# Four of eight heads of the projection as three fp32r products in two of the four slots, with their inputs split on GpSimd, ScalarE and VectorE

## The reference

```python
# branch 1, on the layernorm of x; 16 heads of width 64, INNER = 1024
h1 = adaln(x, t, norm1_w, norm1_b)
x = mha(h1, h1, attn1_wq, attn1_wk, attn1_wv, attn1_wo, attn1_bo) + x
h2 = adaln(x, t, norm2_w, norm2_b)
x = mha(h2, context, attn2_wq, attn2_wk, attn2_wv, attn2_wo, attn2_bo) + x
h3 = adaln(x, t, norm3_w, norm3_b)
x = glu_ff(h3, ff_w1, ff_b1, ff_w2, ff_b2) + x
# mha: q, k, v = projections; out = softmax(q k^T / 8) v per head; out @ wo + bo
# branch 2, on the layernorm of the sum: 8 experts, two per token
out_token = sum(score[e] * (silu(a_e) * g_e @ w2[e].T) for e in top2)
```

## Time and profile before

| | us |
|---|---|
| three runs | 2203.51, 2203.67 (median), 2211.51 |
| the profiled execution | 2204.38 |
| its span | 2202.6 |
| TensorE busy | 2084.2 (95%) |
| ScalarE busy | 1387.8 (63%) |
| VectorE busy | 1283.3 (58%) |
| GpSimd busy | 826.0 (38%) |
| projection, f32 passes (two a head) | 1024 of mean 594 ns |
| granted clock of TensorE over the span | 0.985 |

### The profile page before, as it was taken

One profiled execution on the slowest core, in us unless ns is written; L12 is line 12 of the kernel. 1 busy time (PEld: TensorE's weight loads), 2 busy tenths in 40 slices (PEclk: granted clock), 3 DMA queues, 4 the chain that ended last, 5 costly groups with the idle time before them and its releaser, 6 DMA issues. The chain is left out here.

```text
span 2202.6 us, 37962 instructions
## 1 busy us (share of the span) xinstructions
PE 2084.2 (95%) x11004; PEld 1328.8 (60%) x11004; DVE 1283.3 (58%) x3373; ACT 1387.8 (63%) x2629; POOL 826.0 (38%) x1022
## 2 busy tenths in 40 slices
PE   6899999999999999999999999999999797898896
PEld 5455555555555555555555555555555466788896
DVE  4454656565656565666666665666554744455465
ACT  4566666676757676767675767676666555565564
POOL 1222323334343433342424333333323443556653
PEclk9999999999999999999999999999999898999998
DMA  4110111111111212112121111211114111112256
GB/s 141 48 27 25 49 34 49 49 49 44 48 50 45 59 34 57 45 46 53 38 53 42 49 48 47 59 41 50 39 35 118 43 53 43 51 50 63 61 178 207
DMA packets 134576, 127.73 MB, mean 58 GB/s; under 512 B 14665, under 2 KB 108521, under 8 KB 134442
## 3 DMA queue, kind: packets, MB, share of 16 engines
q1 hardware_dynamic: 125162, 108.03, 17.6%
q0 software_dynamic: 9280, 18.28, 2.5%
HBM read 86.63 MB, written 40.67 MB: 58 GB/s over the span
## 5 line engine op out<-in xcount | busy, mean ns | idle before, releaser
L1795 POOL TENSOR_TENSOR pr<-pr,sm 128x512 f32<-128x512 f32 x256 | 264.3, 1047 | 812.9 <-DVE sm L1355 812.9
L775 PE MATMUL ps<-tt,V 128*128 128x512 f32 x1024 | 502.2, 594 | 3.5 <-ACT tt L1050 3.5
L1050 ACT ACTIVATE kp<-ps 128x512 f32<-128x512 f32 x512 | 294.5, 600 | 198.8 <-PE ps L272 196.1
L1345 DVE TENSOR_REDUCE mx<-ps 128x8 f32<-128x512 f32 x256 | 176.9, 691 | 347.0 <-PE ps L732 346.9
L1050 ACT ACTIVATE tt<-ps 128x512 f32<-128x512 f32 x512 | 275.3, 591 | 42.5 <-PE ps L762 42.2
L732 PE MATMUL ps<-kp,hf 128*64 128x256 f32 x2048 | 279.2, 394 | 14.2 <-DVE pr L1348 11.1
L272 PE MATMUL ps<-cT,M 128*128 128x512 f32 x768 | 267.9, 472 | 0.0
L272 PE MATMUL ps<-hk,M 128*128 128x512 f32 x768 | 249.1, 447 | 1.9 <-DVE hk L1404 1.9
L732 PEld LDWEIGHTS ps<-kp,hf 128*64 128x64 f32 x2048 | 125.5, 137 | 205.4 <-DVE pr L1348 141.0
L1050 ACT ACTIVATE pt<-ps 128x512 f32<-128x512 f32 x256 | 153.7, 600 | 149.9 <-PE ps L744 147.3
L877 PE MATMUL ps<-xT,wt 128*128 128x128 f32 (+1 forms) x1728 | 226.0, 282 | 16.6 <-DVE ux L1610 7.6
(11 more groups left out here) (219 smaller groups left out, 3032.5 us busy)
## 6 DMA issues: line engine op xcount, KB each, us to landing
mod<-emb_s SPq DMA_DIRECT2D x96, 256.0 KB, 4.2
xr<-rows_s SPq DMA_DIRECT2D x144, 66.0 KB
cb<-y_s SPq DMA_DIRECT2D x32, 256.0 KB, 5.1
x_in<-in_x_dram SPq DMA_DIRECT2D x16, 256.0 KB, 4.3
xn_s<-x_in SPq DMA_DIRECT2D x16, 256.0 KB, 2.0
res<-xn_s SPq DMA_DIRECT2D x16, 256.0 KB, 2.7
c_in<-in_ctx_dram SPq DMA_DIRECT2D x16, 256.0 KB, 4.7
y_s<-res SPq DMA_DIRECT2D x16, 256.0 KB, 2.1
```

What stands on the lines that cost most here:

```text
L775: mm = nc.tensor.matmul(psO[:], Vw[a][:, g * HG + head_at(h), :], tt[:, h, :], start=(g == 0 and h == 0), stop=(g == 1 and h == HG - 1))
L1050: return nc.scalar.activation(o, i, ACT.Copy)
L1345: nc.vector.tensor_reduce(mx[:, p % 2, :], heads(psS[p % 2][:]), AX_X, ALU.max).then_inc(max_done, 1)
L1795: tensor(v, v, sm[:, p, :].unsqueeze(2).broadcast_to([P, HG, 64]), ALU.mult).then_inc(prob_done, 1)
```

## The change

Of the eight heads of a unit the last four (HF = 4, HR = 4) become three fp32r products, for units 3 and 0 (RU) only. In the setup their V is stored as hi and lo (Vr) instead of f32. The weighted sums of these heads are split into tt_h and tt_l, 128x4x128 a pair: pairs 0 to 2 by GpSimd (split: a multiplication by ones that writes fp32r, then a subtraction), pair 3 by ScalarE (last_split, behind the second key) and VectorE (last_rest). The split heads are projected in the slot after the unit's, that is in slots 0 and 1. The rest of the change makes room: a semaphore less for the router (rt_rec counts both), for the zero rows (st_rows begins at DM) and for combine (cb_done counts both sums), and the table tb1 lies in the memory of tb2.

```diff
+    HF = HG // 2
+    HR = HG - HF
+            RU = (3, 0)
+            R0 = sa("R0", [P, 2, HR, D], F32R)
+            R3 = sa("R3", [P, 2, HR, D], F32R)
+            Mw, Vw, Vr = [M0, M1], [V0, V1], {0: R0, 3: R3}
+                tt_h, tt_l = (sw(f"tt_{k}", [P, HR, CT], F32R) for k in "hl")
...
# TensorE, project
+                ends = g == 1 and h == HG - 1
+                if u in RU and h >= HF:
+                    if h == HF:
+                        pe.wait_ge(tr_lo, 3 * split_seq(i, u) + 3)
+                        pe.wait_ge(last_lo, split_seq(i, u) + 1)
+                    halves = tt_h[:, h - HF, :], tt_l[:, h - HF, :]
+                    mm = mm3(psO[:], lambda k: Vr[u][:, k, h - HF, :], lambda k: halves[k], first=False, last=ends)
+                else:
+                    mm = nc.tensor.matmul(psO[:], Vw[a][:, g * HG + head_at(h), :], tt[:, h, :], start=(g == 0 and h == 0), stop=ends)
...
# ScalarE: setup copy of a V tile of these units, and the last pair
+                    if unit in RU:
+                        at, src = 2 * (g % 2), ps[:].rearrange("p (a two b) -> p a two b", a=2, two=2)
+                        copy(Vw[a][:, 8 * (g // 2) + g % 2:8 * (g // 2) + 8:4, :], src[:, :, 0, :])
+                        op = copy(Vr[unit][:, 0, at:at + 2, :], src[:, :, 1, :])
+            def last_split(i, u):
+                act.wait_ge(tt_done, t_count(i, u, 3))
+                copy(tt_h[:, :, 3 * P:], tt[:, HF:HG, 3 * P:]).then_inc(last_hi, 1)
+                    if h == 1 and last and lu in RU:
+                        last_split(li, lu)
...
# VectorE
+            def last_rest(i, u):
+                dve.wait_ge(last_hi, split_seq(i, u) + 1)
+                tensor(tt_l[:, :, 3 * P:], tt[:, HF:HG, 3 * P:], f32(tt_h[:, :, 3 * P:]), ALU.subtract).then_inc(last_lo, 1)
+                    if h == 2 and last and lu in RU:
+                        last_rest(li, lu)
...
# GpSimd
+            def split(i, u, p):
+                n = 3 * split_seq(i, u) + p
+                cols = slice(p * P, (p + 1) * P)
+                pool.wait_ge(tt_done, t_count(i, u, p))
+                tensor(tt_h[:, :, cols], tt[:, HF:HG, cols], allone[:].unsqueeze(1).broadcast_to([P, HR, P]), ALU.mult).then_inc(tr_hi, 1)
+                pool.wait_ge(tr_hi, n + 1)
+                tensor(tt_l[:, :, cols], tt[:, HF:HG, cols], f32(tt_h[:, :, cols]), ALU.subtract).then_inc(tr_lo, 1)
+                ahead = int(here and last and lu in RU)
                 for p in range(NT):
                     if u == 2 and p == 1 and ok(i - 3):
                         router_sub(i - 3)
+                    if ahead and p == 3:
+                        prob(i, u, 0)
+                    if last and lu in RU and p >= 1:
+                        split(li, lu, p - 1)
-                    if h < NT and here:
-                        prob(i, u, h)
+                    if h + ahead < NT and here:
+                        prob(i, u, h + ahead)
```

More of the change, by code:

```diff
@@ L261, in pixart_block_moe @@
         ld_cb = [sem(f"ld_cb{q}") for q in range(4)]
-        cb_sum, cb_done = sem("cb_sum"), sem("cb_done")
+        cb_done = sem("cb_done")
         st_cb = [sem(f"st_cb{q}") for q in range(4)]
@@ L352, in seq, with split_seq @@
             return 4 * i - 2 + u
+        def split_seq(i, u):
+            if first(i):
+                return 0
+            if isinstance(i, int) and i == NC:
+                return 2 * NC - 1
+            return 2 * i - (u == 0)
         def rounds(engine, body):
@@ L634, in _ @@
             sp.wait_ge(tb_done, 2)
-            sp.wait_ge(st_rows, 16 * 2 * NT * NC)
+            sp.wait_ge(st_rows, DM + 16 * 2 * NT * NC)
             sp.wait_ge(st_pad, 2 * 16 * E)
@@ L1325, in setup_rest @@
                     _, a, g = tile
-                    op = nc.vector.tensor_copy(Vw[a][:, 8 * (g // 2) + 4 + g % 2:8 * (g // 2) + 8:2, :], ps[:, 2 * P:].rearrange("p (a b) -> p a b", a=2))
+                    unit = 2 * a + g // 2
+                    if unit in RU:
+                        at, src = 2 * (g % 2), ps[:].rearrange("p (a two b) -> p a two b", a=2, two=2)
+                        hi, lo = (Vr[unit][:, k, at:at + 2, :] for k in range(2))
+                        op = tensor(lo, src[:, :, 1, :], f32(hi), ALU.subtract)
+                    else:
+                        op = nc.vector.tensor_copy(Vw[a][:, 8 * (g // 2) + 4 + g % 2:8 * (g // 2) + 8:2, :], ps[:, 2 * P:].rearrange("p (a b) -> p a b", a=2))
                 elif tile[0] == "M":
@@ L1449, in norm4 @@
                 if not first(c):
-                    dve.wait_ge(st_rows, 16 * 2 * NT * c)
+                    dve.wait_ge(st_rows, DM + 16 * 2 * NT * c)
                     dve.wait_ge(hx[3], c)
@@ L1475, in router_dot @@
                 dve.wait_ge(rt_mul, c + 1)
-                nc.vector.tensor_reduce(rt_dot, qk4, AX_X, ALU.add).then_inc(rt_dotted, 1)
+                nc.vector.tensor_reduce(rt_dot, qk4, AX_X, ALU.add).then_inc(rt_rec, 1)
                 dve.wait_ge(rt_tot, c + 1)
@@ L1713, in combine @@
                 dve.wait_ge(ld_cb[q], 48 * nth)
-                tensor(cb[q][0][:], cb[q][0][:], cb[q][1][:], ALU.add).then_inc(cb_sum, 1)
-                dve.wait_ge(cb_sum, done)
+                tensor(cb[q][0][:], cb[q][0][:], cb[q][1][:], ALU.add).then_inc(cb_done, 1)
+                dve.wait_ge(cb_done, 2 * done - 1)
                 tensor(cb[q][0][:], cb[q][0][:], cb[q][2][:], ALU.add).then_inc(cb_done, 1)
```

32 lines of the change are left out of this document (16 added, 16 removed).

## The result

The changed kernel takes 2182.82 us (median of 4 runs, 2181.11 to 2183.79), the kernel before 2203.59 us beside it (4 runs, 2201.70 to 2211.51). The ratio is 0.9902, with a 95% interval of 0.9882 to 0.9922: 20.8 us less. The profiled execution of the changed kernel took 2183.79 us (span 2181.9, mean granted clock 0.987).

A forecast was written before the change was run, and what follows sets the result against it. TensorE's order of work in the attention stage was taken as the bound. 2204.4 - 20.7 (products) + 1.3 (stall) + 0.6 (setup) + 0.2 (end) = 2185.8, stated as 2185.5 us; range for 8 in 10: 2180 to 2197.

The forecast's parts named there:

- What bounds the kernel: Attention stage: the order of TensorE's work is the time; each us removed is gained if nobody it waits for becomes late.
- TensorE saves 0.162 us a head: Projections in slots 0 and 1: a head falls from 0.857 to 0.695 us, four heads, 32 times, 20.7 us in all.
- The rival that the triples don't pay: Projection: triples run at the f32 head's price, 0.162 becomes 0, time 2204 to 2206 us; chance 0.06.
- GpSimd's splits: Slots 0 and 1: two operations a pair, 1.28 us each, 192 in all; no cost on the path.
- The edge: Slot 0: scatters land too late for norm4 above 1.6 us a split operation; TensorE stalls from 1.9.
- The stall in slot 1: last_rest waits for GpSimd's port: TensorE stalls 0 or 0.2 us, taken as 0.1 in 13 chunks, 1.3 us in all.
- when y2 is ready: Slot 1: the tmp sum is ready at 970.2 or 971.3; TensorE wants it at 971.09.
- Slot 1's forecast of 24.8: Sign of being right: TensorE's slot 1 is 24.8 us long instead of 25.36.
- Setup and the ends: Setup: V copies doubled, 0.6 us taken of 0 to 1.5; projecting-only last slot: wait for third split, 0.2 us taken.
- The sum: Whole kernel: 2204.4 - 20.7 + 1.3 + 0.6 + 0.2 = 2185.8 us, stated as 2185.5.
- the second rival: GpSimd's splits far slower than modulate: at 2.1 us an operation the gain is eaten, at 2.3 time 2217; chance 0.07.

The follow-up runs named there:

- Run 2: Changed kernel with the three fp32r products on other fp32r data already there, so no splits and no waits for them: 2153.69 us, ratio 0.9901 to the kernel before.
- run 1: Changed kernel without the three fp32r products: all heads projected in f32 as before, splits still made and waited for: 2174.07 us, ratio 0.9996 to the kernel before.
- run 3: Changed kernel with GpSimd splitting the last pair too, last_split and last_rest taken out: 2159.08 us, ratio 0.9920 to the kernel before.
- run 7: Changed kernel with three operations of 1.28 us instead of two in each GpSimd split: 2228.78 us, ratio 1.0126 to the kernel before.
- run 8: Changed kernel with VectorE making the last pair's rest twice, one after the other: 2196.25 us, ratio 0.9970 to the kernel before.
- run 4: Changed kernel with products and splits in all four slots instead of two: 2210.34 us, ratio 1.0166 to the kernel before.
- run 5: Changed kernel with products and splits in slots 0, 1 and 2, slot 3 left alone: 2218.39 us, ratio 1.0072 to the kernel before.
- 6: Three-slot version; in slot 2 the router's multiplication goes ahead of GpSimd's passes, the last pair's split behind h's: 2193.97 us, ratio 0.9957 to the kernel before.
- 9: Reordered three-slot version, with GpSimd's last two passes in slot 2 held until norm 1 is applied: 2196.32 us, ratio 0.9974 to the kernel before.
- run 11: Reordered three-slot version, with slot 2's last two passes held until norm 1 and its modulation finish: 2146.72 us, ratio 0.9873; changed kernel beside it 2155.07 us.

## Why the prediction was right, point by point

- *What bounds the kernel.* Right, and shown from both sides: the order of TensorE's work is the time as long as nobody is late. Run 2 has the gain without the splits, run 1 the splits without the gain.
- *TensorE saves 0.162 us a head.* Right: 0.69 us a triple, 24.51 us for slot 0 (24.5 forecast), 20.8 to 20.9 us for the stage in two of three executions (20.7 forecast). The rival that the triples don't pay is out. By the 216 ns a product of the Trainium skill ("TensorE: Matmul & The Clock Gate", section "Back-to-back issue gap") slot 0 would be 25.17 - 4 x (0.857 - 0.65) = 24.34 us, an estimate. The prediction took this figure for a stream of products, but the section gives it for a single one by itself and some 131 ns for a stream with weight loads. The trace has 0.230 us a product, near the first and far from the second.
- *GpSimd's splits.* Right: 1.28 us, scatters ended 23.97 us into slot 0 (953.5 - 929.57 = 23.9 forecast), norm4 unhindered. The edge was put at 1.6 us an operation for the scatters and 1.9 for TensorE. The first number fits: with 2.1 us more of GpSimd's work ahead of the scatters (run 3) norm4 is in time, with 3.7 more (run 7) it is 1.48 late, so some 2.2 us are free, an estimate of 0.36 us on each of six operations. The second was mis-sized: run 7, at 3.81 us a pair, stands at that 1.9, and slot 1 is already 1.7 us or more longer in twelve of thirteen chunks. norm4, once late, meets the next split and takes 1.0 us longer, which the estimate left out. Where between 1.64 and 1.9 TensorE begins to stand was not run. The rival's estimate also left out the two ends of the stage, where run 7 lost 10 us.
- *The stall in slot 1*, taken at 0.1 us a chunk (1.3 in all): wrong in size, it is 0 (the two slots of 24.9 us named above lose their 0.2 us ahead of this place, and y2 is still 0.47 us ahead of TensorE in them). The step that failed is when y2 is ready: 15.46 or 16.56 us into the slot was worked out, for a start at the next end of a GpSimd operation and 0.69 us from there, and it is 15.89 in the middle chunks of three executions. last_rest fell into the later of the two cases, behind the first pass, but that pass ended 14.74 us into the slot where 15.16 (969.9 - 954.74) was worked out, and last_rest and y2 ended 0.55 and another 0.60 us behind it instead of 0.69 each. So y2 is 0.46 us ahead of TensorE. That the place is tight and last_rest longer than 0.69 us was right; run 8 shows the price of 1.46 us more. Slot 1's forecast of 24.8 came out at 24.69. What it does cost, GpSimd's three passes at 3.50 instead of 3.05 us, was not forecast and delays nobody that TensorE waits for.
- *Setup and the ends.* The setup is 62.12 us against 60.16, more than the 0.6 taken; but it is 61.51 with V stored as before (run 1) and 60.29 to 62.02 in the other runs with the R tiles, so it scatters by more than the term, and the term stays unmeasured. The last stretch, in which TensorE only projects, went from 17.16 to 16.55 us with no wait for the third split: 0.04 short of the full 0.65, where 0.2 was taken.
- *The sum* of 2185.5 is 2.7 above the median. The stall that did not come is 1.3 of it; the rest is within what the stages of two executions differ by. In three jobs the medians give a saving of 20.8, 25.0 and 22.0 us, where the sum comes to 18.2 below 2203.67: the direction and the size are earned, the last few us are luck. In the second rival, the stall at 2.1 us an operation is 1.4 by its own sum and not 1.6.
- What it did not ask is why two slots and not four. Runs 4, 5, 6, 9 and 11 answer it: in slot 2 the splits fit only if the router's multiplication, the last pair and two passes are moved out of norm 1's way; in slot 3 TensorE stands 1.8 us for VectorE, and it was left alone. Whether it can be ordered too was not tried.

## What to carry to other kernels

Work put on an idle engine is free up to a slack that the timeline shows beforehand: find, in each stage, the one instruction of the idle engine that others wait for (a scatter, a router step), and count the microseconds ahead of it, not the engine's idle share; GpSimd's 50% busy hid slot 0, with some 2.2 us to spare ahead of its scatters, and slot 2 with none. When GpSimd and VectorE both work from SBUF, an operation that meets another can take twice its price, and moving one often moves the collision to the next; hold the movable one back until the whole dependent chain is through. And where an edit pays in some stages and not in others, try each stage alone: all four slots were 35 us slower than before, two 21 to 25 us faster (22 in the job of run 11), and three, in the right order, 30, of which the traces give the third slot less than 2.

## What the runs showed of the hardware

- VectorE and GpSimd hold each other up in both directions. last_rest took 0.74 to 1.47 us in the changed kernel, where a subtraction of that shape with an input in PSUM takes 0.69; norm 1's four steps 1.02, 1.24 or 2.73 us and the four after them 1.14 or 2.69, by how many of GpSimd's passes of 1.05 us ran beside them; three such passes 3.05 or 3.50. The rule of the Trainium skill, "SBUF — State Buffer", section "SBUF: two separate sides", that one of the two stands while the other holds the shared pair, fits this: last_rest ends 0.55 us behind a pass, and then the next pass is 1.50 us long. Which ports were used no trace shows. VectorE's 128x512 subtractions and maxima with an input in PSUM, 0.68 to 0.69 us throughout, are not touched.
- GpSimd writes fp32r at its f32 price (1.28 to 1.29 us for 128x512 with two inputs), and a multiplication by a small broadcast tile of ones costs the same as a subtraction of two full inputs, while the pass over the probabilities, also with a small second input, takes 1.05. What makes that difference is open.
- A stand of TensorE of 2.1 us is followed in some chunks by a stretch at the lower clock level, and the slot is 1.5 us longer (five of twelve chunks in run 4, nine of twelve in run 5). The waits of 1.9, 2.3 and 3.5 us at the ends of the stage in runs 3 and 7, once each, were followed by the lower level too; after stands of 1.2 to 1.3 us (runs 6 and 9) the clock stayed up in all twelve chunks of each.
